# Eight loads in flight instead of four, and branch steps a place later, in a two-layer gated model

## The chip, the cores and the metric

One core of a Trainium2 chip runs the whole program. The metric is device microseconds of one execution; the kernel before took 1480.65 us, the median of three runs (1479.81 to 1485.36). The profiled execution took 1480.23 us, its span is 1478.6 us.

## The reference

Two layers, each a recurrent mixing step and a feed-forward part, both behind a gain:

```python
x = x + tanh(g_xattn[0]) * wkv(w, u, layernorm(x), ctx)
x = x + tanh(g_ffn[0])   * dense(layernorm(x), W1, W2, W3)
x = x + tanh(g_xattn[1]) * wkv(time_decay, time_first, layernorm(x), ctx)
x = x + tanh(g_ffn[1])   * experts(layernorm(x), gate_w, w1, w2, w3)
```

x is 8 x 256 x 512, that is 2048 tokens. `wkv` is a decaying weighted mean over the 256 steps of a sequence: sum of exp(k) v over sum of exp(k), with a bonus for the step itself. `dense` is `silu(x W1') * (x W3')`, 2048 wide, then a Walsh-Hadamard transform and W2. `experts` routes each token to two of eight experts by a gate and adds `silu(h1) * h3` times w2, weighted.

## The kernel before

The tokens are four groups of 512, x lies in SBUF as `X`, four rows of four tiles (a row for each group). All large matmuls are done in f16 with every operand split into a high and a low half, three products each.

**Three parts.** A prologue prepares the dense weights and group 0. Then come 64 *chunks*: chunk n = 16 g + j does slice j of the 2048 hidden columns for group g. An epilogue does the last group's second mixing step and the routing, and then the expert slots run, bound by TensorE.

**A chunk.** TensorE does an A group and a B group of 12 up matmuls each (L983, bank A and bank B), then the 12 down matmuls of the chunk before (L995). ScalarE (ACT) takes silu of bank A into `sg` (L532), VectorE (DVE) multiplies it with bank B (L819, the *product*), ACT casts it to its high half `hs` (L540) and DVE makes the low half (L823). The next A group waits for silu, the next B group for the product, the down group for the low half. Each engine has one instruction order, fixed when the program is built.

**Branches.** Beside the chunks run mixing steps of other groups: `("pre", g)` is the first layer's mixing of group g, `("post", g)` the second layer's. `FIRST` gives a branch's first chunk, F here. `STEPS` gives each step's chunk after F and its place: place 0 is ahead of the chunk's up matmuls and its silu, place 1 is behind them. On DVE both places lie ahead of the product. In order: `stats` (DVE) and `r0` (ACT, logarithm and exponential of the variance), `newton`; `norm` (ACT, writes `A`); `kT0/kT1`, eight transposes each on TensorE (L955); `e0/e1` (ACT, exp); `k0`, `k1`, `den`, `num`, `mix` (DVE, the scans and products; L677 begins k0, L683 k1, L643 den, L637 num, L696 mix); `ln`, `rec` (ACT); `yT0/yT1` (transposes of `V`, L960); `add0/add1` (DVE, with new statistics); `r2`, `newton2`, `norm2`; `xT0/xT1` (L955); `xh`, `xl` (the halves of the result on ACT and DVE); for a post branch `last` (TensorE, the gate's logits, L966) and `raw`, and then the gate steps `gate1`, `gate1b`, `gate2`, `rank`, `ranked` at the chunks of `GATES`. In chunk 16 g + 1 DVE also adds the dense result of group g - 1 to x (`resid`, L831).

**Units.** The experts' weights are 192 *units* of 128 x 512 f32 in DRAM. Each is loaded (SP, L285), cast to its high half by ACT (L433), its low half is made by DVE (L804), and both are stored as f16 (SP, L289). `UNITS` says how many a chunk does. The first of a chunk stands ahead of silu on ACT and ahead of the product on DVE, the second between silu and `hs` and between the product and the low half, the others last. The loads land in `raw`, a ring of four; SP issues in turn the store of unit u and the load of unit u + 4. `LATE` gives the chunks in which a piece of the dense weights is still cast (`w_high`, `w_low`), staged in rows 2 and 3 of `X`, which their x can only enter afterwards.

## Time and profile before

| | us |
|---|---|
| median of three runs | 1480.65 |
| profiled execution | 1480.23 |
| its span | 1478.6 |
| first up matmul of chunk 0 | 111.88 |
| first up matmul of chunk 63 | 732.50 |
| residual add of the last group | 745.62 |

The page says of the whole span: PE 1242.8 us busy (84%), DVE 727.5 (49%), ACT 505.4 (34%), POOL 202.7 (14%). PE's tenths in the 40 slices are lower in the slices of the dense chunks than in those of the expert slots, and its clock is 8 or 9 tenths in many of them. The start times below are microseconds from the span's start. A group of matmuls printed as one row has its start and its length; since matmuls overlap, the pace is to be taken from one start to the next.

### The profile page before, as it was taken

Reading aid. Unit: us, or ns where it says so; the run is one execution under the profiler, and the core shown is the slowest. Engines: PE = TensorE matmul, PEld = TensorE weight load, DVE = VectorE, ACT = ScalarE, POOL = GpSimd, SP = SyncE. Lnnn points to the kernel's source line nnn. Section 1 sums busy time; section 2 is a strip of 40 time slices with the busy share of each in tenths; the row PEclk is TensorE's granted clock in tenths of the full one; section 3 lists DMA queues with packets and bytes.
Section 4 is the critical chain, followed back from the end, with each engine's and each line's share of the span. In section 5 each row is a group of like instructions: output and inputs, shape, how many; then the busy total and the mean of one; then the engine's idle time right before and its main releaser. Section 6 shows DMA issues by size and latency. Waiting matters only on the chain. (4 is left out here: it accounts for less than half of the span.)

```text
span 1478.6 us, 19663 instructions
## 1 busy us (share of the span) xinstructions
PE 1242.8 (84%) x5785; PEld 590.7 (40%) x5786; DVE 727.5 (49%) x1175; ACT 505.4 (34%) x671; POOL 202.7 (14%) x206
## 2 busy tenths in 40 slices
PE   1278798899899898988924099999999999999995
PEld 0034344344454444534513044444444444444442
DVE  6957967868679587795665312122122121221221
ACT  3337557466463675545432011111111111111110
POOL 0000000000003000030200322322122223222232
PEclk9989999999999999999965589999999999999998
DMA  6024577455662656627777078696989896945333
GB/s 253 29 114 162 195 252 260 138 167 173 209 210 58 192 191 213 200 78 246 230 204 238 18 157 197 138 185 147 146 177 191 183 191 146 192 80 102 76 68 61
DMA packets 228344, 239.11 MB, mean 162 GB/s; under 512 B 137168, under 2 KB 141520, under 8 KB 225168
## 3 DMA queue, kind: packets, MB, share of 16 engines
q1 hardware_dynamic: 84816, 163.53, 34.7%
q10 hardware_dynamic: 130512, 52.70, 19.8%
q0 software_dynamic: 12960, 22.15, 8.0%
q8 instruction: 32, 0.52, 0.2%
q14 instruction: 24, 0.20, 0.0%
HBM read 138.68 MB, written 69.65 MB: 141 GB/s over the span
## 5 line engine op out<-in xcount | busy, mean ns | idle before, releaser
L1058 PE MATMUL PS<-weights,xs 128*128 x1872 | 413.1, 381 | 30.0 <-DMA xs<-X 30.0
L983 PE MATMUL PS<-xs,weights 128*128 128x512 f16 x1536 | 359.4, 391 | 27.6 <-DVE sg L819 16.5
L1058 PEld LDWEIGHTS PS<-weights,xs 128*128 128x128 f16 x1872 | 183.8, 98 | 252.9 <-issue 33.9
L983 PEld LDWEIGHTS PS<-xs,weights 128*128 128x128 f16 x1536 | 153.0, 101 | 223.9 <-issue 26.8
L886 DVE SCALAR_TENSOR_TENSOR A<-A,PS 128x1024 f32<-128x1024 f32 x39 | 47.6, 1221 | 349.0 <-PE PS L1058 325.7
L995 PE MATMUL PS<-weights,hs 128*128 128x512 f16 x768 | 182.1, 388 | 1.2 <-DVE hs L823 1.2
L578 ACT ACTIVATE A<-PS 128x1024 f32<-128x1024 f32 x39 | 39.9, 1023 | 322.8 <-PE PS L1058 197.0
L337 POOL DMA_INDIRECT row_list<-entry,pos x32 | 39.6, 1238 | 792.2 <-DVE pos L769 461.4
L804 DVE SCALAR_TENSOR_TENSOR halves<-raw,halves 128x512 f16<-128x512 f32 x192 | 128.9, 686 | 37.9 <-ACT halves L433 37.2
L433 ACT ACTIVATE halves<-raw 128x512 f16<-128x512 f32 x192 | 115.7, 618 | 40.4 <-DMA raw<-ew 37.2
L995 PEld LDWEIGHTS PS<-weights,hs 128*128 128x128 f16 x768 | 76.4, 100 | 88.1 <-issue 7.2
L897 DVE TENSOR_SCALAR V<-PS,outl 128x512 f32<-128x512 f32 x39 | 29.3, 751 | 164.6 <-PE PS L1072 149.4
L1072 PE MATMUL PS<-weights,SQ 128*128 x480 | 106.7, 379 | 0.0
L586 ACT ACTIVATE E<-A 128x1024 f16<-128x1024 f32 x39 | 41.2, 1056 | 189.6 <-DVE A L886 169.0
L1072 PE MATMUL PS<-weights,xs 128*128 x456 | 101.6, 379 | 3.9 <-DMA xs<-E 3.1
L955 PE MATMUL PS<-idn,A 128*128 128x128 f32 x256 | 44.8, 333 | 69.2 <-ACT A L479 63.0
L373 POOL DMA_INDIRECT out<-V,outl x39 | 68.8, 1764 | 199.8 <-DVE V L897 192.4
L540 ACT ACTIVATE hs<-sg 128x512 f16<-128x512 f32 x64 | 40.2, 627 | 142.4 <-DVE sg L819 142.4
L1072 PEld LDWEIGHTS PS<-weights,SQ 128*128 128x128 f16 x480 | 47.0, 98 | 56.6 <-issue 1.0
L955 PEld LDWEIGHTS PS<-idn,A 128*128 128x128 f32 x256 | 37.6, 173 | 78.5 <-issue 67.7
L1072 PEld LDWEIGHTS PS<-weights,xs 128*128 128x128 f16 x456 | 44.5, 98 | 58.4 <-issue 7.4
L1013 PE MATMUL PS<-weights,hads 128*128 128x512 f16 x128 | 32.3, 417 | 41.6 <-DVE weights L789 41.6
(144 smaller groups left out, 1024.3 us busy)
## 6 DMA issues: line engine op xcount, KB each, us to landing
raw<-ew SPq DMA_DIRECT2D x192, 256.0 KB, 3.8
e<-halves SPq DMA_DIRECT2D x192, 256.0 KB, 3.0
weights<-e SPq DMA_DIRECT2D x96, 512.0 KB, 4.8
V<-ctx_cm ACTq DMA_DIRECT2D x7, 1024.0 KB, 5.5
X<-w ACTq DMA_DIRECT2D x4, 1024.0 KB, 6.0
out<-X ACTq DMA_DIRECT2D x4, 1024.0 KB, 9.7
xn_rows<-SQ ACTq DMA_DIRECT2D x8, 512.0 KB, 4.1
X<-w2t SPq DMA_DIRECT2D x3, 1024.0 KB, 10.7
```

The source lines that it names most:

```text
L373: gp.indirect_dma_start(out, bass.IndirectOffsetOnAxis(ap=outl[:, par, 0:1], axis=0), yt[par], None, compute_op=ADD).then_inc(ysto[par], 16)
L433: act.activation(halves[:, u % RING, 0, :], raw[:, u % RING, :], ACT.Copy, scale=SW).then_inc(s["unit_hi"], 1)
L540: act.activation(hs[:, n % 2, 0, :], sg[:, n % 2, :], ACT.Copy).then_inc(s["hh_done"], 1)
L578: act.activation(sil[0], h1, ACT.Silu, scale=1.0 / (SW * SX)).then_inc(s["sil_done"], 1)
L586: act.activation(hid[par][:, :, 0, :], act8, ACT.Copy).then_inc(s["aT_used"], 1)
L804: ve.scalar_tensor_tensor(halves[:, u % RING, 1, :], raw[:, u % RING, :], SW, halves[:, u % RING, 0, :], MUL, SUB).then_inc(s["unit_lo"], 1)
L886: ve.scalar_tensor_tensor(sil[1], sil[0], SH / (SW * SX), h3, MUL, MUL).then_inc(s["act_done"], 1)
L955: ins = te.transpose(bank(S0 + c - a)[:, i * P:(i + 1) * P], A1[:, i * D + c * P:i * D + (c + 1) * P], idn[:, :])
L983: ins = te.matmul(bank(bk), wj[:, j, w, a, c * P:(c + 1) * P], xs[:, g % 2, b, c, :], start=(k == 0 and c == 0), stop=(k == 2 and c == C - 1))
L995: ins = te.matmul(bank(OUT0 + i), hs[:, n % 2, b, i * P:(i + 1) * P], wj[:, j, 2, a, :], start=j == 0 and k == 0, stop=j == J - 1 and k == 2)
L1058: ins = te.matmul(bank(n), xTt[k][:, b, c, :], weights_of(off, 2 * I // NT * c + n, a), start=(c == 0 and m == 0), stop=(c == C - 1 and m ...
L1072: ins = te.matmul(bank(6 + k % 2), aTt[k][:, b, c, :], weights_of(off, 2 * C * I // U + c, a), start=(c == 0 and m == 0), stop=(c == IC - ...
```

## The change

Four things are edited. The places of units (`unit_places`, new): besides the four of `raw`, four tiles of row 3 of `X` are lent from the end of chunk 9 until chunk 26, and four of row 0 from chunk 31 on, when group 0 is done with them. Each unit's load goes to the place that has been free the longest, and is issued by SP behind the store of the unit that was there, or the first time behind the last store of the chunk that frees it. SP's loop is unrolled, and x of group 3 is loaded by SP behind the last unit that used row 3, where ACT had issued it. `UNITS` is a new table; no unit stands ahead of silu any more, the first comes between silu and `hs`, all others last. `STEPS`: norm, kT0, k0, yT0, xT0, xT1, the x halves, last and raw come one place or one chunk later. `FIRST`, `GATES` and `LATE` are moved to match.

```diff
-FIRST = {("pre", 1): 0, ("pre", 2): 11, ("post", 0): 20, ("pre", 3): 30, ("post", 1): 39, ("post", 2): 49}
-GATES = {0: (31, 32, 34, 34, 35), 1: (50, 51, 53, 53, 54), 2: (60, 61, 62, 61, 62)}
-LATE = {1: 2, 2: 3, 4: 4, 7: 5, 9: 6, 10: 7}
+FIRST = {("pre", 1): 0, ("pre", 2): 10, ("post", 0): 20, ("pre", 3): 30, ("post", 1): 39, ("post", 2): 49}
+GATES = {0: (34, 40, 41, 42, 43), 1: (53, 58, 59, 59, 59), 2: (61, 62, 63, 63, 63)}
+LATE = {1: 2, 2: 3, 4: 4, 6: 5, 8: 6, 9: 7}
...
-STEPS = [("stats", 0, 0), ("r0", 0, 0), ("newton", 0, 0), ("norm", 1, 0), ("kT0", 1, 1), ("e0", 2, 0), ("k0", 2, 0),
+STEPS = [("stats", 0, 0), ("r0", 0, 0), ("newton", 0, 0), ("norm", 1, 1), ("kT0", 2, 0), ("e0", 2, 0), ("k0", 3, 0),
...
-         ("yT0", 6, 1), ("add0", 7, 0), ("yT1", 7, 1), ("add1", 8, 0), ("r2", 8, 0), ("newton2", 8, 0), ("norm2", 8, 1),
-         ("xT0", 9, 0), ("xh0", 9, 0), ("xl0", 9, 0), ("xT1", 9, 1), ("xh1", 10, 0), ("xl1", 10, 0), ("last", 10, 1),
-         ("raw", 11, 0)]
+         ("yT0", 7, 0), ("add0", 7, 0), ("yT1", 7, 1), ("add1", 8, 0), ("r2", 8, 0), ("newton2", 8, 0), ("norm2", 8, 1),
+         ("xT0", 9, 1), ("xh0", 10, 0), ("xl0", 10, 0), ("xT1", 10, 1), ("xh1", 11, 0), ("xl1", 11, 0), ("last", 11, 1),
+         ("raw", 12, 0)]
...
+LEND, LENT, GIVEN = max(LATE), 26, 31
+
+def unit_places():
+    done = list(itertools.accumulate(n for row in UNITS for n in row))
+    last = [-1] * RING + [done[LEND] - 1] * 4 + [done[GIVEN] - 1] * 4
+    uses, places = [0] * (RING + 8), []
+    for u in range(NU):
+        open_ = [k for k in range(RING + 8) if last[k] < u - 1 or k < RING]
+        if u >= done[LENT]:
+            open_ = [k for k in open_ if not RING <= k < RING + 4]
+        k = min(open_, key=lambda k: (last[k], k))
+        places.append((k, uses[k], last[k]))
+        uses[k], last[k] = uses[k] + 1, u
+    return places
...
-            with sp.Fori(0, NU // RING - 1, 1) as m:
-                for k in range(RING):
-                    store_unit(RING * m + k, k)
-                    load_unit(RING * m + RING + k, k)
+            def load_units(ahead):
+                for u, (k, use, after) in enumerate(PLACES):
+                    if after == ahead:
+                        if k == RING and use == 0:
+                            sp.wait_ge(s["w_lo"], NW)
+                        if k == RING + 4 and use == 0:
+                            sp.wait_ge(s["x3_out"], 16)
+                        sp.dma_start(raws[k], ew[u * P:(u + 1) * P, :]).then_inc(unit_in[k], 16)
+            for u in range(NU):
+                sp.wait_ge(s["unit_lo"], u + 1)
+                sp.dma_start(e16[u * P:(u + 1) * P, :], ...).then_inc(unit_out[u % RING], 16)
+                load_units(u)
+                if u == lent:
+                    sp.dma_start(xg(3), x_tm[3, :, :]).then_inc(x_in[3], 16)
...
                 if n in LATE:
                     w_high(LATE[n])
-                for u in units[0:1]:
-                    unit_high(u)
                 act.activation(sg[:, n % 2, :], bank(ABANK), ACT.Silu, ...)
                 for step in steps_beside(g, j, 1):
                     run(*step)
-                for u in units[1:2]:
+                for u in units[0:1]:
                     unit_high(u)
...
                 act.activation(hs[:, n % 2, 0, :], sg[:, n % 2, :], ACT.Copy)...
-                for u in units[2:]:
+                for u in units[1:]:
                     unit_high(u)
```

DVE's chunk is edited in the same way. The units of a branch's chunks F + 2 to F + 6 were 4, 4, 1, 2, 4 for post 0 and are 4, 0, 3, 4, 4.

TensorE, chunks 28 to 30, before (L983 is the up group of a chunk, L995 a down group, L955 are xT0 and xT1 of post 0, L966 its logits):

```order
L983 MATMUL PS<-xs,weights 128x512 x24
L995 MATMUL PS<-weights,hs 128x512 x12
L955 MATMUL PS<-idn,A 128x128 x8
L983 MATMUL PS<-xs,weights 128x512 x24
L955 MATMUL PS<-idn,A 128x128 x8
L995 MATMUL PS<-weights,hs 128x512 x12
L983 MATMUL PS<-xs,weights 128x512 x24
L966 MATMUL PS<-gw,E 128x8 x16
```

The same chunks after, with L1005, L1017 and L977 for the three kinds:

```order
L1005 MATMUL PS<-xs,weights 128x512 x24
L1017 MATMUL PS<-weights,hs 128x512 x12
L1005 MATMUL PS<-xs,weights 128x512 x24
L977 MATMUL PS<-idn,A 128x128 x8
L1017 MATMUL PS<-weights,hs 128x512 x12
L1005 MATMUL PS<-xs,weights 128x512 x24
L977 MATMUL PS<-idn,A 128x128 x8
L1017 MATMUL PS<-weights,hs 128x512 x12
```

xT0 moved behind the up group of chunk 29, xT1 behind that of chunk 30, and the logits are in chunk 31.

ACT, from silu of chunk 38 to silu of chunk 40, before (L532 silu with its table, L479 the norm, L433 units, L540 `hs`, L504 a half of x, L452 to L464 the logarithm step of post 1):

```order
L532 ACTIVATE sg<-PS 128x512
L479 ACTIVATE A<-X,rt 128x512 x4
L433 ACTIVATE halves<-raw 128x512
L540 ACTIVATE hs<-sg 128x512
L504 ACTIVATE xs<-PS 128x1024
L452 ACT_TABLE_LOAD
L463 ACTIVATE rt<-mv,eps 128x4
L464 ACTIVATE rt<-rt 128x4
L433 ACTIVATE halves<-raw 128x512
L532 ACT_TABLE_LOAD
L532 ACTIVATE sg<-PS 128x512
```

After, from the second silu (chunk 39) to the norm behind silu of chunk 40 (L557 silu, L460 units, L565 `hs`, L544 and L545 the exponentials of gate1b, L531 a half of x, L506 the norm of post 1):

```order
L557 ACTIVATE sg<-PS 128x512
L460 ACTIVATE halves<-X 128x512
L565 ACTIVATE hs<-sg 128x512
L460 ACTIVATE halves<-X 128x512 x3
L544 ACT_TABLE_LOAD
L544 ACTIVATE q<-q 128x32
L545 ACTIVATE q<-q 128x32
L531 ACTIVATE xs<-PS 128x1024
L557 ACT_TABLE_LOAD
L557 ACTIVATE sg<-PS 128x512
L506 ACTIVATE A<-X,rt 128x512 x4
```

The unit ahead of silu is gone, the exponentials and a half of x stand ahead of silu of chunk 40, and the norm came behind it.

DVE, from the units behind the low half of chunk 22 to the product of chunk 24, before (L804 units, L677 and the first L637 are k0, L683 to L643 k1, L819 the product, L823 the low half, the last two den):

```order
L677 TENSOR_TENSOR V<-E,V 128x1024
L637 SCALAR_TENSOR_TENSOR SQ<-dec,E 128x256 x4
L804 SCALAR_TENSOR_TENSOR halves<-raw,halves 128x512
L819 SCALAR_TENSOR_TENSOR sg<-sg,PS 128x512
L804 SCALAR_TENSOR_TENSOR halves<-raw,halves 128x512
L823 TENSOR_TENSOR hs<-sg,hs 128x512
L804 SCALAR_TENSOR_TENSOR halves<-raw,halves 128x512 x2
L683 TENSOR_TENSOR V<-E,V 128x1024
L637 SCALAR_TENSOR_TENSOR SQ<-dec,E 128x256 x4
L643 SCALAR_TENSOR_TENSOR E<-E,eu,SQ 128x2x255 x2
```

After (L828 units, L701 and the first L661 are k0, L707 to L667 k1, L841 and L845 product and low half of chunk 23):

```order
L828 SCALAR_TENSOR_TENSOR halves<-raw,halves 128x512 x3
L701 TENSOR_TENSOR V<-E,V 128x1024
L661 SCALAR_TENSOR_TENSOR SQ<-dec,E 128x256 x4
L707 TENSOR_TENSOR V<-E,V 128x1024
L661 SCALAR_TENSOR_TENSOR SQ<-dec,E 128x256 x4
L667 SCALAR_TENSOR_TENSOR E<-E,eu,SQ 128x2x255 x2
L841 SCALAR_TENSOR_TENSOR sg<-sg,PS 128x512
L845 TENSOR_TENSOR hs<-sg,hs 128x512
L667 SCALAR_TENSOR_TENSOR E<-E,eu,SQ 128x2x255 x2
L661 SCALAR_TENSOR_TENSOR A<-dec,V 128x256 x6
```

k0 moved from ahead of chunk 22's product to k1, and the units between are gone.

## Rows read from the trace of the kernel before

**Rows 1.** Windows: busy time per engine, granted clock, DMA share, GB/s.
```profile
core 0: us, PE busy (x) PEld busy (x) DVE busy (x) ACT busy (x) POOL busy (x), PEclk, DMA share, GB/s
111.00:746.00 635.00, 572.23 (x2712) 277.12 (x2712) 471.66 (x821) 364.09 (x517) 31.49 (x24) 0.95 0.58 187
```

**Rows 2.** Timeline of PE: start us, length us, line, operands; chunk starts and pace.
```profile
111.88 5.35 PE L983 MATMUL PS<-xs,weights 128*128 128x512 f16 x24 [3.21 <-DVE weights L799]
...
311.71 7.03 PE L983 MATMUL PS<-xs,weights 128*128 128x512 f16 x24
...
500.23 6.68 PE L983 MATMUL PS<-xs,weights 128*128 128x512 f16 x24
...
592.22 1.04 PE L955 MATMUL PS<-idn,A 128*128 128x128 f32 x8
593.09 2.75 PE L995 MATMUL PS<-weights,hs 128*128 128x512 f16 x12
595.68 5.34 PE L983 MATMUL PS<-xs,weights 128*128 128x512 f16 x24
600.86 3.63 PE L966 MATMUL PS<-gw,E 128*128 128x8 f32 x32
...
732.50 5.34 PE L983 MATMUL PS<-xs,weights 128*128 128x512 f16 x24
```

**Rows 3.** Waits of PE, 115 to 746: us in total, times, longest.
```profile
PE PS L955 <- ACT A L479: 22.2, 8, 5.1
PE PS L983 <- DVE sg L819: 16.5, 13, 2.5
PE PS L960 <- DVE V L697: 12.4, 6, 4.6
PE PS L983 <- ACT sg L532: 7.9, 3, 4.3
```

**Rows 4.** ACT's units (L433): duration ns, and what ACT waited for.
```profile
L433 ACT ACTIVATE halves<-raw x192: 612/615/631, 116.8 to 744.4; 128x512 f16<-128x512 f32 x192
...
  DMA raw<-ew: 37.2, 20
```

**Rows 5.** Timeline of DVE: scan steps of post 0, then gate1.
```profile
343.57 1.22 DVE L683 TENSOR_TENSOR V<-E,V 128x1024 f32<-128x1024 f32 x1 [1.72 <-ACT E L490]
...
347.30 1.41 DVE L643 SCALAR_TENSOR_TENSOR E<-E,eu,SQ 128x510 f32<-128x510 f32 x2
...
352.48 1.41 DVE L643 SCALAR_TENSOR_TENSOR E<-E,eu,SQ 128x510 f32<-128x510 f32 x2
...
357.43 0.69 DVE L804 SCALAR_TENSOR_TENSOR halves<-raw,halves 128x512 f16<-128x512 f32 x1
...
360.44 1.27 DVE L637 TENSOR_TENSOR_SCAN A<-dec,V 128x256 f32<-128x256 f32 x2
...
369.49 2.28 DVE L696 SCALAR_TENSOR_TENSOR SQ<-E,SQ 128x2048 f32<-128x2048 f32 x1
...
372.96 1.22 DVE L698 TENSOR_TENSOR V<-V,SQ 128x1024 f32<-128x1024 f32 x1
...
419.46 0.18 DVE L712 COPY q<-PS 128x32 f32<-128x32 f32 x1
...
422.14 0.69 DVE L804 SCALAR_TENSOR_TENSOR halves<-raw,halves 128x512 f16<-128x512 f32 x1
```

**Rows 6.** Timeline: from the stats to silu in chunk 20; half of xn.
```profile
314.11 0.68 DVE L630 BATCH_NORM_STATS2 st<-X 128x6 f32<-128x512 f32 x1
...
317.42 1.28 ACT L452 ACT_TABLE_LOAD   x1 [4.48 <-DVE mv L631]
...
319.78 1.28 ACT L532 ACT_TABLE_LOAD   x1
...
321.08 0.60 ACT L532 ACTIVATE sg<-PS 128x512 f32<-128x512 f32 x1
...
400.44 1.90 ACT L508 ACTIVATE SQ<-A 128x2048 f16<-128x2048 f32 x1
```

**Rows 7.** Timeline of DVE: the last group's residual add.
```profile
745.62 2.34 DVE L831 SCALAR_TENSOR_TENSOR X<-PS,sc,X 128x2048 f32<-128x2048 f32 x1
```

38 lines of the change are left out of this document (16 added, 22 removed), and 6 rows, old and new, of the table UNITS.

## The prediction

> **What bounds the kernel now.** I read the windows first. The kernel has three parts: the 64 dense chunks (111 to 746 us), an epilogue that belongs to one branch alone, and the expert slots. The dense part is 635 us of the span and PE is busy in 572 of them at a granted clock of 0.95 [rows 1]. The changed lines all lie in it, apart from names; so the sum is made there. Next the pace of PE: 24 up matmuls take 5.18 us from first start to the next group's start, eight transposes 0.87, twelve down matmuls 2.59 [rows 2]. A chunk at full rate is therefore 5.18 + 2.59 = 7.77 us, a branch adds six groups of transposes (5.2 us), and each of the three gates' logit matmuls 3.5 (600.86 to the next group). Then the chunk starts [rows 2] against that pace. From chunk 0 to 20 there are 20 chunks, less the down group that chunk 0 lacks, and 11 transposes: 155.4 - 2.6 + 9.6 = 162.4, measured 199.8, lost 37.4. From 20 to 39 (12 transposes, one logit group): 147.6 + 10.4 + 3.5 = 161.5, measured 188.5, lost 27.0. From 39 to 49 (7): 77.7 + 6.1 = 83.8, measured 95.5, lost 11.7. From 49 to 63 (6, two logit groups): 108.8 + 5.2 + 7.0 + 0.4 = 121.4, measured 136.8, lost 15.4. All told 91 us are lost. The waits of PE explain 60 of them: transposes of A on the norm 22.2, of V on mix 12.4, up matmuls on the gate product (`sg`) 16.5, and on silu 7.9 [rows 3]. The rest is mostly the half clock behind a wait: 24 matmuls that take 5.34 us at 2.4 GHz take 7.03 at 311.71 and 6.68 at 500.23, behind transposes that had waited on the norm [rows 2]; so one such drop to 1.2 GHz costs 1.3 to 1.7 us in the up group alone. So PE bounds the dense part, and what counts is how late ACT and DVE are at these four hand-overs. ACT's own waits for raw units, 37.2 us in 20 places [rows 4], hurt only where it has no slack.
>
> **Part 1, transposes a place later.** Each transposed group now stands behind 5.18 or 2.59 us more of matmuls, and nothing is added to PE. The norm waits (22.2, longest 5.1) for xT0 go: the norm follows silu at once on ACT and is shorter than the up group of 5.18 that now lies between. Of the V waits (12.4) 2.6 us each are covered. But `k0` moves from chunk F+2 (F is the first chunk of a branch) into F+3, beside `k1`. With DVE's prices [rows 5] I follow one branch. k0 is a product and four scans, as k1's first two rows, 3.73 (343.57 to 347.30). k1 takes 5.06 (343.57 to 352.48, less a `sg`, an `hs` and four units at 0.61 each and a wait of 0.2), den 4.95 (352.48 to 357.43), num 6.40 (360.44 to 369.49, less `sg`, `hs`, two units and the wait, 2.65), mix 4.6 (3.5 to the second half's product at 372.96, when the first half of V is ready, and 1.15 for that). DVE is free about 1.4 us into F+3 (three units behind `hs`); k0 and k1 end at 10.2, and `sg` must end by 5.18 + 5.18 to keep the next B group in time: 0.45 late. F+4 (den) is in time, having 3 units instead of the four on both sides of before. F+5: 20.6 + 6.40 = 27.0 against a product that may start at 25.7: 1.3 late. F+6 has had four units behind it: V's half is ready at 34.4, PE is there at 32.8: 1.6. Two small ones follow, 0.4 (yT1 on the add) and 0.6 (silu behind `r2`). That is 4.35 us a branch, and DVE, not PE, paces F+3 to F+6, so a half clock inside it is mostly absorbed. Before, the same branch at 25 to 29 waited longer and clocked down twice.
>
> **Part 2, no unit before silu.** A unit of 0.62 on ACT [rows 4] goes from in front of silu, and one like it on DVE from in front of `sg`. It is worth 0.6 us only in a chunk where silu or `sg` ends last. Those are the first chunks of the branches: stats from 314.11 until ACT goes on at 317.42 (3.3), then table load, logarithm, unit, table load and silu, which ends at 321.68 [rows 6]: 4.27 us, now 3.65. The unit is not dropped, it comes behind `hs`, where it lies beside matmuls.
>
> **Part 3, what the new places collide with.** At F+10 the transposed halves (`xh0`, `xl0`) now stand in the same place as the next branch's stats and r0, in front of silu. Behind a pre branch these are 1024 elements on either engine, half of what takes 1.9 and 2.3 us, and cost 1 us of stall (chunk 20). Behind a post branch ACT has 1.0 + 1.9 [rows 6] and DVE 2.3 (as mix's first row [rows 5]) ahead of the stats: ACT is done at 2.9, DVE with its low half at 5.2, the stats end at 8.5, silu 3.65 later at 12.1, while PE gets to the next A group at 5.18 + 0.87 + 2.59 = 8.65. Stall 3.4 at chunk 30; 4.4 at 49, where the residual add of 2.3 [rows 7] stands too; each with a half clock of 1.7. At 39 nothing lies between `r2` of one branch (chunk 38) and the next's stats: silu of chunk 38 ends as chunk 39 starts, then come norm2 (four slices, 2.9 as an estimate from 1.9 for 2048 elements and a start-up each), a unit, `hs`, the low half and two units, so DVE is free at 6.2, + 3.3 + 3.65 = 13.1 against 8.7: stall 4.3 again. And `gate1b` of post 0 in front of silu in chunk 40 adds the exponentials, two table loads of 1.28 and a chain of eight small DVE operations (1.8, by gate1's twelve in 2.7, 419.46 to 422.14 [rows 5]), so that the norm behind it ends 3.1 us after kT0 is due (half clock included). In the first ten chunks the weight staging comes a chunk earlier: w_high (1.9) and w_low (2.3) fall beside den, mix and `r2`. Followed with the same prices, DVE's chain gives stalls of 0.75, 1.65, 0.55, 0.95, 0.55 and 1.45 at chunks 4 to 8. Then silu of chunk 8 has `r2` (add1 ends 4.9, + 1.85), w_high 1.9, table and silu in a row, 10.6 against 7.8: 2.8 at chunk 9; 1.0 at 10, where w_high waits for its piece, issued only behind chunk 8; and with that lateness and the next branch's stats 4.6 at 11.
>
> **Part 4, eight places for raw units.** A load has eight units of lead instead of four, some two chunks, so ACT's 37.2 us of raw waits go once the lent rows are in use (after chunk 9). On PE's way this is little: most of it lies beside matmuls. The clear gain is at the end: the residual add of the last group starts at 745.62, 13.1 after chunk 63's start [rows 2, 7], while 5.18 + 2 x 2.59 and the last units put it at 10.5; the units stand in front of `hs` and of the add and come late with their loads. Gain 2.6. Issuing the loads unrolled and queueing two row loads of X behind them on SP I price at 0; if a store had to wait behind such a load, at most a few us once, and a gain there has no mechanism.
>
> **The sum.** Lost after: 0 to 20: 3.3 (chunk 0: wait 1.6 with half clock) + 5.9 (to chunk 8) + 8.4 + 1.7 x 2 + 6.6 (pre 2, with the residual add in chunk 17) + 1.4 half clock = 29.0, saves 8.4. 20 to 39: 1.0 + 4.35 + 3.4 + 1.7 + 0.9 (half clock behind the logits) + 8.0 (pre 3: the residual add 2.35 and gate1 2.7 join the scans) + 1.0 = 20.3; one transposed group fewer falls in the stretch (0.9): saves 7.5. 39 to 49: 4.3 + 3.1 + 7.1 + 0.7 = 15.2: costs 3.5. 49 to 63: 4.4 + 1.7 + 0.9 + 7.4 + 0.7 + 1.7 + 1.0 = 17.8, and one group of transposes more: costs 3.3. End: saves 2.6. Net 8.4 + 7.5 - 3.5 - 3.3 + 2.6 = 11.7. The profiled execution took 1480.23 us (span 1478.6), 0.4 under the median of the three runs; 1480.65 - 11.7 = 1469. Epilogue and expert slots keep their time.
>
> **A rule of the Trainium skill weighed.** In this trace a table load takes 1.28 us and the silu behind it starts 0.02 later [rows 6]; the instruction order has four more of them now, all about gate1b, at chunks 40 and 58. The Trainium skill ("ScalarE: Activation LUTs", What ACT_TABLE_LOAD costs) puts a switch at 1.28 plus a drain of 1.38. By that page the four switches would cost 5.5 us more on ACT, of which about 3 reach PE at 40 and 58, and the time would be 1472. The row shows no such drain, so I go by the row.
>
> **Rivals.**
> Full slack. DVE and ACT are less late than I add up, and the moved transposes and the loads' lead take away the 22.2 + 12.4 us of waits for the norm and for V [rows 3] with most of their half clock, while the new collisions cost only half of my 20 us. For it: these are the two largest of the removable waits. Against it: DVE's scan chain has barely slack. Gain 25, time 1455.
> No change. The stalls only change their names: the norm waits become silu waits one chunk on. For it: at 39 PE goes on without a silu wait, but at its start it had waited on the norm, up to 5.1 us [rows 3], so that silu had that much more time. If each of the six scan chains runs 1 us later than I say, 6 us of the 12 are gone: 1475.
> Slower. The mechanism is the logarithm in front of silu in the crowded chunks 10, 30, 39, 40 and 49. If DVE reaches the stats 2 us later there than I say (units of the chunk before, four instead of three), each stall grows by 2 and draws a half clock of 2.5 instead of 1.7, and kT0 behind it waits as well: 5 x (2 + 0.8 + 0.8) = 18 more, 1487. It decides from 3.3 us a chunk on.
> A longer table switch. If a table load holds ACT longer than its row says, the four added ones come late in front of silu at 40 and 58: 1472 by the Trainium skill's drain, of which no row speaks.
>
> **Chances.** Forecast 1469 (1462 to 1476): 0.55. Full slack 0.13, no change 0.15, slower 0.14, the page's 0.03. A measurement of this kernel tells about 0.5% from no change, that is below 1473.2 or above 1488.1. Forecast's own spread puts three quarters under 1473.2: faster 0.42 + 0.13 = 0.55, same 0.13 + 0.12 + 0.03 + half of the slower case (it ends at 1487 with as much below as above 1488) 0.05 = 0.33, slower 0.12 with the tails. Range 1455 to 1484, which leaves out about 2 in 10.
>
> **What would show it.** Right: no PE wait on the norm over 1 us save kT0 at chunk 41; PE waits on silu grow from 3 to some eight, at chunks 1, 9 to 11, 31, 40, 50 and 59, sum over 20 us; waits on V stay at five or six with about 1.6 each; raw waits of ACT under 10 us; granted clock of 111 to 735 about 0.95 or a little above; residual add 10.5 after chunk 63 starts. Wrong: if silu waits at 31, 40 and 50 are missing (full slack), or if `sg` waits in F+4 exceed 2 us in every branch (DVE chain underrated).

## The result and the profile after

The changed kernel took 1499.89 us (median of five runs, 1496.72 to 1502.1), the one before 1485.36 (five runs, 1479.81 to 1488.54): a ratio of 1.0108, 95% interval 1.0084 to 1.0132. It is 1.1% slower, where 1469 us was forecast. The profiled execution has a span of 1498.3 us, 19.7 more than before. The medians are only 14.5 apart: the profiled execution of before (1480.23) was one of its faster ones, so some 5 of the 19.7 us are chance.

The windows first. The dense part now lasts until 764.65 us instead of 745.62. PE is busy in it for 2.3 us less than before [rows 1] with as many matmuls, and its clock is a shade higher, so all of the loss is waiting.

```profile
111.00:765.00 654.00, 569.94 (x2712) 273.12 (x2712) 471.77 (x823) 368.80 (x524) 22.90 (x20) 0.96 0.58 182
```

The waits of PE and of ACT's units, 115 to 762 us (in total, times, longest):

```profile
PE PS L1005 <- ACT sg L557: 33.3, 11, 5.8
ACT halves L460 <- DMA e<-halves: 27.9, 13, 8.3
PE PS L1005 <- DVE sg L841: 13.2, 13, 2.0
PE PS L982 <- DVE V L721: 12.3, 6, 5.6
PE PS L977 <- DVE xs L733: 8.9, 3, 7.1
ACT halves L460 <- DMA raw<-ew: 5.1, 4, 1.9
PE PS L993 <- ACT E L533: 4.9, 1, 4.9
```

Against [rows 3] the 22.2 us on the norm are gone, and those on silu grew from 7.9 to 33.3. Against [rows 4] ACT's 37.2 us for raw units are 5.1, but it now waits 27.9 for its *stores* (e from halves). And two waits are new in kind: transposes of A on `xs` (L733, the low half of a branch's result), and the rank matmuls (L993) on `E`. Both are waits for the engine that still reads the two side PSUM banks. The rank step was also moved, which the list of the change does not say: in `GATE_STEPS` it went from place 1 to place 0, ahead of its chunk's up matmuls.

All of PE's waits come to 81.1 us here, and to 60.2 before (115 to 746). The four hand-overs that the prediction reckoned with (norm, V, product, silu) are 58.8 of them, and were 59.0 [rows 3]. So the norm's waits were traded for silu's, and the growth in sum lies outside the four: 22.3 us instead of 1.2. Of these, 19.3 are waits for a reader of the side banks (8.9 on `xs`, 7.1 on `E`, 3.3 on the add, which reads yT0).

PE's timeline holds the chunk starts of [rows 2] (chunks 0, 20, 39, 49 and 63 are the first, second, third, eighth and last row) and the worst place:

```profile
113.54 5.35 PE L1005 MATMUL PS<-xs,weights 128*128 128x512 f16 x24 [3.21 <-DVE weights L823]
...
300.15 5.34 PE L1005 MATMUL PS<-xs,weights 128*128 128x512 f16 x24
...
487.77 5.35 PE L1005 MATMUL PS<-xs,weights 128*128 128x512 f16 x24 [0.44 <-ACT sg L557]
...
500.59 7.04 PE L1005 MATMUL PS<-xs,weights 128*128 128x512 f16 x24 [4.01 <-ACT sg L557]
...
520.01 1.97 PE L977 MATMUL PS<-idn,A 128*128 128x128 f32 x8 [7.12 <-DVE xs L733]
521.77 6.82 PE L1005 MATMUL PS<-xs,weights 128*128 128x512 f16 x24
...
534.30 0.18 PE L993 MATMUL PS<-a,tris 128*128 128x8 f16 x1 [2.25 <-ACT E L517]
...
602.48 5.34 PE L1005 MATMUL PS<-xs,weights 128*128 128x512 f16 x24
...
617.09 6.93 PE L1005 MATMUL PS<-xs,weights 128*128 128x512 f16 x24 [5.81 <-ACT sg L557]
...
752.46 5.35 PE L1005 MATMUL PS<-xs,weights 128*128 128x512 f16 x24
```

So 0 to 20 takes 186.6 us (before 199.8), 20 to 39 187.6 (188.5), 39 to 49 114.7 (95.5) and 49 to 63 150.0 (136.8); DVE's residual add starts 12.2 after chunk 63 (13.1, [rows 7]):

```profile
764.65 2.35 DVE L853 SCALAR_TENSOR_TENSOR X<-PS,sc,X 128x2048 f32<-128x2048 f32 x1 [1.06 <-PE PS L1017]
```

Chunk 0 starts 1.7 us later, and what follows the add takes 733.7 instead of 733.0. The sum: -13.2 - 0.9 + 19.2 + 13.2 - 0.9 + 1.7 + 0.7 = 19.8, but for rounding the difference of the spans. All of the loss lies behind chunk 39, apart from 9 us at 30 to 33 that 33 to 39 and 20 to 30 give back.

**Chunk 30** takes 14.3 us (392.43 to 406.75), because its silu is late. ACT's last two units of chunk 29 wait 1.26 and 1.28 us for their loads, so ACT is done with its part of `xh0` at 397.41, 5.0 us into the chunk instead of the 2.9 forecast, and DVE, which waits for it, begins `xl0` and the stats only then:

```profile
394.07 0.63 ACT L460 ACTIVATE halves<-raw 128x512 f16<-128x512 f32 x1 [1.28 <-DMA raw<-ew]
...
397.44 2.29 DVE L728 SCALAR_TENSOR_TENSOR SQ<-A,SQ 128x2048 f16<-128x2048 f32 x1 [2.02 <-ACT SQ L535]
```

At chunk 49 ACT is as late, behind two units that wait 0.86 and 1.27 us for stores.

**Chunk 40** (500.59 to 521.77, 21.2 us where 7.8 is full pace) shows two more causes, the side banks and the gate in front of silu. ACT, then DVE:

```profile
503.55 1.28 ACT L544 ACT_TABLE_LOAD   x1
506.22 0.23 ACT L544 ACTIVATE q<-q 128x32 f32<-128x32 f32 x1 [1.38 <-DVE q L767]
...
506.48 1.00 ACT L531 ACTIVATE xs<-PS 128x1024 f16<-128x1024 f32 x1
507.50 1.28 ACT L557 ACT_TABLE_LOAD   x1
508.79 0.60 ACT L557 ACTIVATE sg<-PS 128x512 f32<-128x512 f32 x1
510.39 2.93 ACT L506 ACTIVATE A<-X,rt 128x512 f32<-128x512 f32 x4 [1.00 <-issue]
...
515.83 1.00 ACT L531 ACTIVATE xs<-PS 128x1024 f16<-128x1024 f32 x1
```

```profile
516.89 0.18 DVE L779 TENSOR_TENSOR q<-q 128x32 f32<-128x32 f32 x1
...
518.73 1.23 DVE L733 SCALAR_TENSOR_TENSOR xs<-PS,xs 128x1024 f16<-128x1024 f32 x1
```

The gate's exponentials with two table loads and the first half `xh0` stand ahead of silu (508.79), norm and `hs` behind it, and only then, in front of chunk 41's silu, comes `xh1` at 515.83; on DVE `gate2` (516.89) stands ahead of `xl1`, which ends at 519.96. PE could have filled kT0 of post 1 from 513.3 on, when the norm that it reads ended, but there are only two side PSUM banks, S0 and S1, for all transposes and gate matmuls: kT0 goes into them when `xl1` has read xT1 out of them. PE stood from 512.9 to 520.0, of which the norm alone would have cost 0.4.

**The stores.** When the last gate step knows a group's places in the routing, GpSimd (POOL) issues eight indirect DMAs, the *scatter*: 1024 entries of 8 bytes into `row_list`. In the changed kernel:

```profile
546.12 1.52 POOL L364 DMA_INDIRECT row_list<-entry,pos  x1 [545.49 <-DVE pos L793]
...
556.27 1.42 POOL L364 DMA_INDIRECT row_list<-entry,pos  x1 [0.30 <-issue]
```

The second group's begin at 712.89. The windows behind the two, and the DMA issues in 540 to 575 and in 575 to 610 (KB each, median us from issue to landing):

```profile
557.00:572.00 15.00, 10.62 (x49) 4.42 (x47) 10.85 (x12) 3.09 (x6) 0.69 (x1) 1.00 1.07 135
725.00:740.00 15.00, 13.58 (x77) 7.63 (x76) 3.21 (x5) 1.89 (x3) 0.00 (x0) 1.00 1.12 129
```

```profile
e<-halves SPq DMA_DIRECT2D x7, 256.0 KB, 8.6
...
e<-halves SPq DMA_DIRECT2D x14, 256.0 KB, 3.1
```

The DMA engines are fully busy and move 129 to 135 GB/s; a store takes 8.6 us instead of 3.1. In the first window the packets of q1, the queue of the units, take 105.5% of the 16 engines' time for 2.02 MB, the scatter's own (q0) 1.1%:

```profile
q1 hardware_dynamic: 1106, 2.02, 105.5%
```

So it is the units' packets that get long. ACT stands at those two places, with the next silu queued behind its units (at 569.36 and 741.08):

```profile
568.83 0.63 ACT L460 ACTIVATE halves<-X 128x512 f16<-128x512 f32 x1 [2.42 <-DMA e<-halves]
...
734.55 0.63 ACT L460 ACTIVATE halves<-X 128x512 f16<-128x512 f32 x1 [8.30 <-DMA e<-halves]
```

### The profile page after: what moved, and what is told of

The parts are those of the page before. It is cut to its first block and busy times, and to the rows that moved or that the text cites. A ratio compares the mean times of both kernels' runs of the same rounds, so it can differ in the third digit from the quotient of the medians.

```text
span 1498.3 us, 18666 instructions
## 1 busy us (share of the span) xinstructions
PE 1245.2 (83%) x5785; PEld 588.5 (39%) x5786; DVE 726.0 (48%) x1175; ACT 508.7 (34%) x675; POOL 198.8 (13%) x206
## 5 line engine op out<-in xcount | busy, mean ns | idle before, releaser
L1005 PE MATMUL PS<-xs,weights 128*128 128x512 f16 x1536 | 360.2, 392 | 49.7 <-ACT sg L557 33.3
L1005 PEld LDWEIGHTS PS<-xs,weights 128*128 128x128 f16 x1536 | 152.1, 100 | 246.0 <-ACT sg L557 38.7
L1017 PE MATMUL PS<-weights,hs 128*128 128x512 f16 x768 | 180.6, 386 | 1.5 <-DVE hs L845 1.5
L602 ACT ACTIVATE A<-PS 128x1024 f32<-128x1024 f32 x39 | 39.9, 1023 | 309.2 <-PE PS L1080 211.9
L364 POOL DMA_INDIRECT row_list<-entry,pos x32 | 35.6, 1113 | 815.3 <-DVE pos L793 545.5
L1017 PEld LDWEIGHTS PS<-weights,hs 128*128 128x128 f16 x768 | 76.2, 100 | 89.3 <-issue 5.2
L828 DVE SCALAR_TENSOR_TENSOR halves<-raw,halves 128x512 f16<-128x512 f32 x116 | 76.7, 685 | 30.5 <-ACT halves L460 30.5
L977 PE MATMUL PS<-idn,A 128*128 128x128 f32 x256 | 41.6, 316 | 55.0 <-ACT A L506 39.9
L565 ACT ACTIVATE hs<-sg 128x512 f16<-128x512 f32 x64 | 40.1, 627 | 138.4 <-DVE sg L841 133.4
L841 DVE SCALAR_TENSOR_TENSOR sg<-sg,PS 128x512 f32<-128x512 f32 x64 | 43.7, 683 | 72.6 <-PE PS L1005 53.2
L460 ACT ACTIVATE halves<-raw 128x512 f16<-128x512 f32 x116 | 68.4, 617 | 11.6 <-DMA e<-halves 6.5
L1094 PEld LDWEIGHTS PS<-weights,xs 128*128 128x128 f16 x456 | 45.3, 99 | 59.9 <-issue 9.4
L1035 PE MATMUL PS<-weights,hads 128*128 128x512 f16 x128 | 33.4, 427 | 41.6 <-DVE weights L813 41.6
```

The costliest lines, as they stand in the source:

```text
L460: act.activation(halves[:, u % RING, 0, :], raws[PLACES[u][0]], ACT.Copy, scale=SW).then_inc(s["unit_hi"], 1)
L565: act.activation(hs[:, n % 2, 0, :], sg[:, n % 2, :], ACT.Copy).then_inc(s["hh_done"], 1)
L828: ve.scalar_tensor_tensor(halves[:, u % RING, 1, :], raws[PLACES[u][0]], SW, halves[:, u % RING, 0, :], MUL, SUB).then_inc(s["unit_lo"], 1)
L841: ve.scalar_tensor_tensor(sg[:, n % 2, :], sg[:, n % 2, :], SH / (SW * SX), bank(BBANK), MUL, MUL).then_inc(s["hid_done"], 1)
L977: ins = te.transpose(bank(S0 + c - a)[:, i * P:(i + 1) * P], A1[:, i * D + c * P:i * D + (c + 1) * P], idn[:, :])
L1005: ins = te.matmul(bank(bk), wj[:, j, w, a, c * P:(c + 1) * P], xs[:, g % 2, b, c, :], start=(k == 0 and c == 0), stop=(k == 2 and c == C - 1))
```

## The experiments

Sixteen kernels were run. "After" is the changed kernel. Ratios are to the kernel before on the same chip, with 95% intervals; before's medians there were 1483.8 to 1485.7. The stretches are differences between the starts of A groups in each profile; "tail" is from chunk 63 to the residual add, "rest" what follows. They are of one profiled execution each, the time is a median. e12 and e15 are the same up to e15's first scatter (452.64), and differ by up to 1.7 us in the stretches before it: less than 2 us in a stretch says nothing.

| | us | ratio | 0-20 | 20-30 | 30-33 | 33-39 | 39-42 | 42-49 | 49-52 | 52-58 | 58-60 | 60-63 | tail | rest |
|---|---|---|---|---|---|---|---|---|---|---|---|---|---|---|
| before | 1485.4 | | 199.8 | 96.8 | 30.2 | 61.5 | 28.5 | 67.0 | 30.2 | 61.6 | 21.5 | 23.5 | 13.1 | 733.0 |
| after | 1499.9 | 1.0108 | 186.6 | 92.3 | 39.4 | 55.9 | 46.8 | 68.0 | 38.6 | 54.0 | 24.3 | 33.1 | 12.2 | 733.7 |
| e1 | 1509.8 | 1.0177 | 185.7 | 93.2 | 39.1 | 56.2 | 46.3 | 71.0 | 41.0 | 55.0 | 24.2 | 34.9 | 13.8 | 733.0 |
| e2 | 1481.4 | 0.9975 | 199.7 | 96.6 | 30.2 | 62.1 | 28.5 | 66.6 | 30.2 | 62.3 | 22.7 | 23.6 | 10.6 | 731.7 |
| e3 | 1491.6 | 1.0049 | 186.6 | 87.2 | 42.5 | 55.9 | 46.2 | 64.5 | 35.0 | 54.0 | 24.1 | 31.1 | 12.2 | 733.6 |
| e4 | 1497.5 | 1.0084 | 186.9 | 92.1 | 39.5 | 55.9 | 39.9 | 68.6 | 40.3 | 54.1 | 24.7 | 34.5 | 12.2 | 733.5 |
| e5 | 1498.6 | 1.0084 | 189.4 | 91.7 | 37.2 | 55.9 | 40.5 | 68.3 | 40.2 | 54.0 | 27.0 | 32.6 | 12.2 | 733.5 |
| e6 | 1504.9 | 1.0113 | 186.7 | 92.7 | 39.6 | 72.3 | 40.5 | 60.9 | 40.5 | 68.6 | 19.0 | 28.7 | 10.6 | 733.3 |
| e7 | 1494.8 | 1.0055 | 186.4 | 87.6 | 38.2 | 56.1 | 45.3 | 69.3 | 40.2 | 54.0 | 24.6 | 31.5 | 12.2 | 733.2 |
| e8 | 1488.0 | 1.0016 | 189.5 | 90.2 | 39.4 | 61.9 | 41.6 | 61.5 | 40.2 | 60.5 | 18.1 | 27.0 | 10.6 | 731.7 |
| e9 | 1488.2 | 1.0016 | 186.6 | 92.6 | 39.8 | 55.9 | 46.6 | 62.2 | 40.1 | 54.5 | 24.3 | 27.0 | 10.6 | 737.6 |
| e10 | 1484.6 | 0.9985 | 189.6 | 90.1 | 38.9 | 60.4 | 35.6 | 61.5 | 40.8 | 59.0 | 18.1 | 28.7 | 10.6 | 738.4 |
| e14 | 1477.2 | 0.9958 | 199.4 | 96.7 | 30.2 | 58.3 | 28.5 | 66.6 | 28.5 | 61.2 | 22.7 | 23.5 | 10.6 | 734.1 |
| e13 | 1487.2 | 1.0004 | 190.3 | 94.4 | 28.5 | 59.7 | 37.1 | 73.8 | 30.2 | 58.1 | 27.5 | 27.4 | 12.2 | 735.5 |
| e11 | 1471.5 | 0.9912 | 187.0 | 102.2 | 30.2 | 58.8 | 28.5 | 69.0 | 28.5 | 60.7 | 21.5 | 23.5 | 10.6 | 737.9 |
| e12 | 1463.7 | 0.9852 | 190.2 | 94.6 | 28.5 | 59.4 | 28.0 | 68.1 | 28.5 | 57.4 | 21.4 | 23.7 | 10.6 | 737.8 |
| e15 | 1471.1 | 0.9915 | 191.7 | 93.5 | 30.2 | 64.0 | 27.6 | 67.9 | 28.5 | 60.0 | 21.7 | 23.7 | 10.6 | 734.0 |
| e16 | 1461.3 | 0.9849 | 190.2 | 94.7 | 28.5 | 59.4 | 27.9 | 68.0 | 28.5 | 59.6 | 22.0 | 23.7 | 10.6 | 734.1 |

### Tables or ring: e1 and e2

e1 is after with the old ring of four raw units; e2 is after's twelve places with all tables and unit places of before.

```
e1: RING = 4 loads as before;  UNITS, STEPS, FIRST, GATES, LATE of after; no unit ahead of silu
e2: PLACES, load_units of after;  UNITS, STEPS, FIRST, GATES, LATE of before; first unit ahead of silu
```

> The changed kernel's tables (steps, first chunks, gates, units, no unit ahead of silu) with the old ring of four places. Theory S (the new step places cost the time: the half-products of x and the gate steps hold the two side banks and stand in front of silu at chunks 30 to 31, 39 to 42, 49 to 50): still slower than before by 10 to 16 us, chunk 40 about 21 us long; ACT waits for raw loads again (30 to 40 us) instead of for stores. Theory R (eight loads in flight push the stores back, and ACT waits for stores): at most 3 us slower than before, store waits under 8 us, since loads and stores alternate again.

Measured 1.0177 (1.0143 to 1.0212), 24 us over before and so more than either theory had; raw waits 51.4 us in 30 places.

> The kernel before with the lent places alone: its tables, its first unit ahead of silu, but eight places for raw units and the unrolled issue. Theory S: 0 to 5 us faster than before, raw waits of ACT under 8 us, store waits below 10. Theory R: 6 to 12 us slower than before, ACT's waits for stores 20 us or more.

Measured 0.9975 (0.9956 to 0.9995): the tail falls from 13.1 to 10.6 us as Part 4 had it. The tables lose 1.8% with the old ring and 1.3% with the places; the places give 0.7% back with them and 0.25% without. In e2 ACT still waits 14.6 us for stores, which before's trace does not show; e14 below, the same kernel with the scatters late, has no such wait.

### Who must wait for a store: e3 and e7

e3 shares the eight lent places, four for raw units and four for halves:

```
-raws = [raw ...] + X rows 3 and 0, tiles 0-3
+raws = [raw ...] + X rows 3 and 0, tiles 0,1;  halves = [halves ...] + X rows 3 and 0, tiles 2,3
```

> The changed kernel, with each lent row shared out: two tiles to raw units, two to the stores' halves, so six places for either. Theory R: the store waits of 27.9 us nearly vanish (under 6) and the time falls by 8 to 13 us against the changed kernel, most at chunks 45, 61 and 62. Theory S: 2 to 5 us faster than the changed kernel at most, chunk 40 stays at 21 us. If the DMA engines themselves are the limit when a chunk does four units, the waits only turn into raw waits of the same sum.

Measured 1.0049 (1.0026 to 1.0073). That is 8.3 us less than after, the low end of theory R. The store waits are gone, and twelve waits for loads, 24.6 us, took their place (after has 5.1). The longest, 10.8 us at 728.91, is where after waited for its stores behind the second scatter:

```profile
ACT halves L474 <- DMA raw<-ew: 12.7, 9, 5.4
ACT X L474 <- DMA X<-ew: 11.9, 3, 10.8
```

e7 is after with the first unit ahead of silu and of the product again.

> The changed kernel with the first unit of each chunk in front of silu and of the gate product again and the second behind silu, as before; tables and the lent places stay as changed. Theory B (with no unit in front, up to three units stand in a row behind the high half of the hidden rows, and their stores come due together, so ACT waits for the store of four units ago): ACT's waits for stores fall from 27.9 us to under 12 in sum and the longest from 8.3 to under 3, but each of the crowded first chunks gets 0.6 later; sum: 2 to 5 us faster than the changed kernel in chunks 42 to 49 and 60 to 63, 2 slower elsewhere; 1495 to 1498. Rival (the store waits come from loads queued eight ahead and not from the bunching): waits for stores stay above 20 us and the first chunks get later, 1501 to 1504.

Measured 1.0055 (1.0032 to 1.0079), faster than after, but not for the reason given: the store waits rose to 44.4 us in 20 places (115 to 790). Its gain is at 20 to 30 (87.6 us against 92.3). So taking the first unit from in front of silu and of the product, which is Part 2, cost time here; why is not settled.

### The side banks and the halves: e4 and e5

```
e4: ("xh1", 11, 0), ("xl1", 11, 0) -> ("xh1", 10, 1), ("xl1", 10, 1)
e5: e4 and ("xh0", 10, 0), ("xl0", 10, 0) -> ("xh0", 9, 1), ("xl0", 9, 1)
```

> The changed kernel with one step moved back: the second half of x (xh1, xl1) stands behind silu of chunk F+10 and no longer in chunk F+11. Theory S: kT0 of post 1 in chunk 41 no longer waits 7.1 us for xl1; chunk 40 shrinks from 21.2 to 15 to 17 us, and 4 to 8 us are saved against the changed kernel; chunk 30 and 49 stay long (14.3, 14.6). Rival: the norm, which ends at 513.2 of that chunk, and DVE's backlog are what kT0 would wait for next: under 2 us saved.

Measured 1.0084 (1.0057 to 1.0112). The bank's wait goes and 39 to 42 falls by 6.9; kT0 of post 1 now waits 1.4 us, on the norm. From 42 to 63 the kernel gives 4.2 back, while its store waits grow from 27.9 to 33.5. The time is 2.4 us less, which the intervals do not tell from after:

```profile
ACT halves L460 <- DMA e<-halves: 33.5, 17, 9.7
...
PE PS L977 <- DVE xs L733: 1.6, 1, 1.6
```

> The changed kernel with the halves of the transposed rows of each branch earlier: the first (xh0, xl0) behind silu of chunk F+9 instead of in front of silu of F+10, the second (xh1, xl1) behind silu of F+10 instead of in front of silu of F+11. Nothing else is moved. Theory C (crowded first chunks: the halves stand in front of the next branch's stats and logarithm in chunks 10, 20, 30, 40, 49): silu of chunks 30 and 49 ends about 3 us sooner after the chunk's start (14.3 and 14.6 in the changed kernel), the wait of the next up group falls from 5.5 and 5.8 to 2 to 3, and chunks 30 to 33 and 49 to 52 fall from 39.4 and 38.6 us by about 4 each; with the side banks free in time as well (chunks 39 to 42 fall from 46.8 to about 40, as with xh1 alone), the time falls by 10 to 14 us against the changed kernel, to about 1487. Rival: the lateness is the vector engine's own backlog and only moves; then chunks 30 to 33 and 49 to 52 keep their 39 us, the halves delay the gate product of chunks F+9 by 1 to 2 us, and the time is 1495 to 1500.

Measured 1.0084 (1.0057 to 1.0111), as the rival had it: 30 to 33 falls by 2.2 only, 49 to 52 rises. The silu waits at chunks 31 and 50 do shrink, from 5.5 and 5.8 us to 3.4 and 2.6, but others come: kT0 of post 1 waits 3.3 on the norm, yT0 7.1 on mix. Taking the halves alone out of the first chunk's way does not mend it.

### The gates: e6, and all three at once: e8

```
-GATES = {0: (34, 40, 41, 42, 43), 1: (53, 58, 59, 59, 59), 2: ...}
+GATES = {0: (32, 33, 35, 35, 36), 1: (51, 52, 54, 54, 55), 2: ...}
```

> The changed kernel with the gates of posts 0 and 1 put right behind their logits again (chunks 32 to 36 and 51 to 55 instead of 34 to 43 and 53 to 59); the rest is as changed. Theory G (the gates are what fills chunks 40 to 43 and 58 to 60): chunk 40, 21.2 us in the changed kernel, loses the two table loads, two exponentials and eight small operations in front of its silu, some 6 us, and the wait of chunk 42 for the rank (2.25) and of 59 (4.9) go; chunks 39 to 42 fall from 46.8 to about 39 and 58 to 60 from 24.3 to 22; chunks 33 to 39 and 52 to 58 grow by about 2 each; time down by 5 to 7, to about 1493. Rival (side banks and the second branch's scans decide, gates only add where there is room): chunk 40 still waits for the low half of xT1 in chunk 41, 39 to 42 falls by less than 3 us, and 33 to 39 and 52 to 58 grow by as much as is won: 1498 to 1502.

Measured 1.0113 (1.0066 to 1.016). 39 to 42 and 58 to 60 fell by 6.3 and 5.3 as expected, 42 to 49 by 7; but 33 to 39 and 52 to 58 grew by 16.4 and 14.6. The gate steps now stand beside k0 and k1, the product of chunk 34 keeps PE waiting for 5.0 us, and the scatter begins at 471.53. (The rank step keeps its new place 0.) The windows and ACT's rows of the kernel with the gates back, then PE's:

```profile
480.00:490.00 10.00, 10.00 (x52) 4.92 (x51) 3.88 (x8) 1.38 (x3) 2.94 (x4) 1.00 1.08 100
490.00:500.00 10.00, 1.87 (x9) 0.67 (x7) 4.03 (x6) 1.03 (x2) 0.00 (x0) 0.83 1.15 85
```

```profile
486.47 0.63 ACT L460 ACTIVATE halves<-X 128x512 f16<-128x512 f32 x1 [7.79 <-DMA e<-halves]
```

```profile
504.22 2.31 PE L1005 MATMUL PS<-xs,weights 128*128 128x512 f16 x5 [12.35 <-ACT sg L557]
```

Here the picture showed itself: behind the scatter, in chunks 37 and 38 here and in 44, 45, 60 and 61 of after, DMA is full at 85 to 135 GB/s, the stores come late, and the silu behind the units with them. That is theory D.

> The changed kernel with three edits at once: the lent rows shared between raw units and halves (two places each), the halves of the transposed rows earlier, and the gates right behind their logits. If the three causes are separate their savings add: 8 (store waits) + 10 (halves early, banks free) + 4 (gates) = 22 less than the changed kernel's 1499, so about 1477, 0.5% faster than before and the fastest of all. If they overlap, as store waits came back when the halves alone were moved, half of that: 1488, slower than before. Chunks 39 to 42: 46.8 us in the changed kernel, 34 or less if additive; 30 to 33: 39.4, 35 or less; 49 to 52: 38.6, 33 or less.

e8 joins e3, e5 and e6. 1487.99 us, 1.0016 (0.9994 to 1.0038): the savings overlap. Against the additive case it is 11 us late, and PE's longest wait on silu, behind chunk 39 and just after the scatter, is 11.0.

### The scatters: e9, e10 and e14

```
+gp.wait_ge(s["resid_done"], NG)      # GpSimd, ahead of the scatters
 for g in range(NG):
     scatter(g)
```

> The changed kernel with the routing list's scatters (eight indirect DMAs of tiny packets for each group of tokens, issued on GpSimd as soon as a group's places are known) all held back until the last residual add; nothing else is moved. In the changed kernel the scatters of posts 0 and 1 are issued at 546 to 557 us and at 713 to 725, and for 10 to 15 us after each the DMA engines are 0.9 to 1.5 busy at only 76 to 200 GB/s, and the scalar engine waits 6.2 and 14.1 us for stores. Theory D (the store waits of chunks 44 to 46 and 60 to 62 come from the scatters, whose place moved with the gates): both go; waits for stores fall from 27.9 us to under 10, chunk 45 falls from 16.0 us to about 11.5, chunks 42 to 49 from 68.0 to about 64, chunks 60 to 63 from 33.1 to 26 to 28, and the time falls by 7 to 12 us to about 1489; the epilogue hides the 31 us of scatters issued late. Rival (the stores bunch behind the high half of the hidden rows whatever the scatters do): waits for stores stay above 20 us and the time within 3 us of 1499; if the late scatters reach the expert slots, the part after the last residual add grows from 734 us by up to 25 and the time with it.

Measured 1.0016 (0.9991 to 1.0041), 0.9% under after. Windows at the same places of chunks 44 and 60, and the waits, of after with the scatters late:

```profile
556.00:571.00 15.00, 13.13 (x65) 6.12 (x64) 14.59 (x17) 4.34 (x8) 0.00 (x0) 1.00 0.58 192
720.00:735.00 15.00, 15.00 (x85) 8.51 (x85) 9.53 (x25) 6.48 (x11) 0.00 (x0) 1.00 0.65 226
```

```profile
PE PS L1006 <- ACT sg L558: 32.8, 11, 6.4
...
ACT halves L461 <- DMA e<-halves: 10.5, 10, 3.7
```

The same queues move 192 GB/s at a share of 0.58 and 226 at 0.65, against 135 at 1.07 and 129 at 1.12. In the first window the units' queue needs 57.8% of the engines' time for 2.88 MB:

```profile
q1 hardware_dynamic: 1588, 2.88, 57.8%
```

A store issued in 540 to 575 lands after 2.9 us there. 42 to 49 falls by 5.8, 60 to 63 by 6.1, and the rest grows by 3.9, where 24 late scatter DMAs now stand ahead of the last group's eight; e16 bears that out. The longest wait on V, 5.6 us, is 1.5. Nothing else was moved, so theory D is shown for after. The silu waits stay, they have another cause, and so do 10.5 us of store waits.

> The combined kernel (lent rows shared, halves earlier, gates right behind their logits) with the scatters held back until the last residual add. The combined kernel's scatters begin at 471 us, and behind them the scalar engine waited 2.2 and 4.9 us for raw units in chunk 39, which took 19.9 us; its stats were 5 us late. Theory D: chunk 39 falls to about 14.5 and chunk 50's wait stays; time 1480 to 1483, about before's. Rival: chunk 39 is late for the vector engine's own backlog; within 2 us of 1488.

0.9985 (0.9961 to 1.0009): 39 to 42 falls from 41.6 to 35.6 and the rest grows by 6.7. The time lies between theory and rival, and its interval overlaps with that of e8.

> The kernel with the tables and unit places of before and the twelve raw places (1481.4 us, run earlier) with the scatters held back until the last residual add. Theory D says what before paid for its own scatters at 461 and 649 us: ACT's unit waits of 7.4 and 6.4 us behind them go, of which PE sees 2 to 4 (chunks 33 to 39 and 52 to 58, 62 us each), and the part after the last residual add grows by 4 to 6 as it did in the changed kernel: 1481 to 1484, no gain. Rival (the scatters cost before as much as the changed kernel, 11 us): 1474 to 1477.

1477.19 us, 0.9958 (0.9941 to 0.9976), against 0.9975 of e2; the intervals overlap. 33 to 39 falls from 62.1 to 58.3, the rest grows from 731.7 to 734.1. From chunk 0 to the last residual add it takes 6.9 us less than e2 (626.2 against 633.1), where e9 takes 11.0 less than after (640.1 against 651.1). No gain was expected: the places of before pay for their scatters too, less than after's, but more than theory D had allowed, and the time is just outside the rival's range.

### The ends of the branches: e13, e11 and e12

e13 undoes one part of after, the places from xT0 on:

```
-("xT0", 9, 1), ("xh0", 10, 0), ("xl0", 10, 0), ("xT1", 10, 1), ("xh1", 11, 0), ("xl1", 11, 0), ("last", 11, 1), ("raw", 12, 0)
+("xT0", 9, 0), ("xh0", 9, 0), ("xl0", 9, 0), ("xT1", 9, 1), ("xh1", 10, 0), ("xl1", 10, 0), ("last", 10, 1), ("raw", 11, 0)
```

> The changed kernel with one part of it undone: xT0, its halves, xT1, its halves, the logits and the raw step of every branch at the places of before (F+9 to F+11). The later norm, kT0, k0 and yT0, the gates at 34 to 43 and 53 to 59, the units and their twelve places, and the scatters right behind the routing stay as changed. Theory (the ends of the branches lose by running into the next branch's first chunks, apart from gates and scatters): 30 to 33 falls from 39.4 us to 28 to 31, 49 to 52 from 38.6 to 28 to 31, 39 to 42 from 46.8 to 36 to 39 (the gate's exponentials are still in front of silu in chunk 40), while the waits of xT0 on the norm come back at chunks 28, 38, 47 and 57 (about 4 us and a half clock each: 20 to 30, 33 to 39, 42 to 49 and 52 to 58 grow by 2 to 4 each); stores still wait 20 us or more behind the scatters. Time 1480 to 1486. Rival (the gates and scatters are the whole loss): 30 to 33 and 49 to 52 stay above 36 and the time at 1495 to 1500.

1487.17 us, 1.0004 (0.9981 to 1.0026), 1.0% under after and 1 us over its range. The waits of PE, 115 to 752 us:

```profile
PE PS L977 <- ACT A L506: 28.5, 7, 7.8
...
PE PS L1005 <- ACT sg L557: 5.7, 5, 1.6
```

30 to 33, 39 to 42 and 49 to 52 fall by 29.0 together, but about 16 of these are lost again in other stretches (1499.9 to 1487.2 is 12.7). Silu waits fall from 33.3 to 5.7 and norm waits come back with 28.5: between these two the waits only change their name. The four hand-overs come to 59.0 us, as in before and in after. What is gained are PE's other waits, the side banks' above all: 11.1 us instead of 22.3.

e11 keeps after's places for the first three branches only (post 0 up to its second norm), with the scatters late.

> The changed order for the first three branches only (pre 1, pre 2, and post 0 up to its second norm); from there and for pre 3, posts 1 and 2 the places of before, gates as before, each chunk's first unit in front of silu as before, raw units in the twelve places, units of the chunks adapted, and the scatters held back. Theory (the change's gain and loss are separate: 13 us won in the first twenty chunks, 4.5 in the next ten, and the loss all in the branch ends at 30, 39, 40 and 49 and the gates): chunks 0 to 20 take 187 us (before 199.8), 20 to 30 90 (96.8), 30 to 33 31 to 34, from 39 on as before; the time is 1462 to 1468. Rival (ACT and DVE are simply behind: what is won early is lost at the next branch, since units and staging left over must be done later): from 30 on it is 10 us longer than before, 1475 to 1480.

1471.54 us, 0.9912 (0.9878 to 0.9946), over the 1462 to 1468 expected. 0 to 20 takes 187 us, and from 30 to 63 it is as before within 3 us; but 20 to 30 takes 102.2, and PE waits 6.1 us on the norm in chunk 29. Four units a chunk stand beside mix and the add there; that this is the cause was not tested.

e12 has for every branch after's places up to norm2 and before's from xT0 on, gates as before, e3's sharing, units moved away from F+3 and the gates, and the scatters late.

> For every branch the changed places up to the second norm (norm, kT, k0, yT a place later) and those of before from xT0 to raw, gates as before, lent rows shared, units of the chunks adapted, scatters held back. Theory (the later transposes of the halves xT0 and xT1, which put the halves and the raw step into the next branch's first chunks, are the part that loses; the later kT0 and yT0 are the part that gains): 0 to 20 187 to 190 us, 30 to 33 32 to 35, 33 to 39 57 to 60, 39 to 42 31 to 34, 49 to 52 31 to 34, 52 to 58 56 to 59; time 1463 to 1472. Rival (the later k0, beside k1, collides with the gates there as it did in the kernel with the gates put back, 12 us at chunk 39 and 5 at 34): 1480 to 1490.

1463.7 us, 0.9852 (0.9812 to 0.9893), within its range. Its dense part and its waits, 115 to 726 us:

```profile
111.00:725.00 614.00, 558.54 (x2712) 272.65 (x2712) 471.74 (x823) 361.77 (x520) 0.00 (x0) 0.97 0.58 194
```

```profile
PE PS L994 <- ACT A L523: 27.2, 6, 7.9
PE PS L1022 <- DVE sg L858: 13.0, 12, 2.0
PE PS L999 <- DVE V L738: 5.2, 4, 1.5
...
PE PS L1022 <- ACT sg L574: 3.1, 3, 1.6
ACT halves L477 <- DMA raw<-ew: 2.7, 2, 2.0
```

Against e13 it lacks the gates in front of silu, among others: 39 to 42 is 9.1 less, 58 to 60 6.1. No store is waited for.

Against before the dense part is 23.2 us shorter, and only 8.4 of that are waits of PE (51.8 instead of 60.2). The same 2712 matmuls keep PE busy for 558.5 us instead of 572.2 [rows 1], at a granted clock of 0.97 instead of 0.95: some 14 us are matmuls that took longer before, at the lower clock. Which of the waits that went had drawn the clock down was not separated.

### When to scatter: e15 and e16

```
e15: e12 without the wait
e16: gp.wait_ge(s["down_done"], 41); scatter(0); scatter(1); gp.wait_ge(s["unit_lo"], NU); scatter(2), scatter(3)
```

> The fastest kernel so far (1463.7 us: first halves of the branches as changed, their ends and the gates as before, lent rows shared) with the scatters again right behind the routing instead of held back. Theory D: they start near 450 and 630 us, beside 4 units a chunk; stores and loads slow down for 10 to 15 us each, ACT waits 5 to 10 us more, 33 to 39 and 52 to 58 grow by 3 to 8 each, and the end gains the 4 back: 1464 to 1472. Rival (with two places more for units and halves nothing waits for the scatters): 1460.

0.9915 (0.9896 to 0.9933), 1471.07 us, as theory D had it; 33 to 39 grows by 4.6, 52 to 58 by 2.6, the rest falls by 3.8.

> The same fastest kernel with the first group's scatters released in chunk 42, where no unit stands, the second's right behind its routing (chunk 54, after two chunks without units), and the others when the last unit is converted. If the late scatters cost 4 us after the last residual add because 24 of them stand in front of the last group's, that part falls from 737.8 to about 733.5 us, and the dense part keeps its time within 1: 1459 to 1461. Rival: the scatters slow the units of chunks 43 and 55 and win nothing: 1463 to 1467.

1461.31 us (1460.29 to 1462.5), 0.9849 (0.983 to 0.9868): the fastest kernel, 1.5% under before. It has the rest back (734.1), and 52 to 58 gives 2.2 of it up again; the intervals don't tell it from e12.

## Why the prediction was wrong

**What bounds the kernel**: right that PE does. But its four hand-overs carry 59.0 of the 60.2 us of waits before and 58.8 of 81.1 after: reckoning by them alone could not see the loss. (The scatters sit in both: e9 has 5.5 us less in the four and 2.7 less outside.) Against the same pace the prediction had 29.0, 20.3, 15.2 and 17.8 us lost in its four stretches; the trace has 24.2, 27.0, 30.9 and 27.7.

**Part 1**, right in its mechanism. The norm waits went. Waits on V were to be five or six of 1.6 each; they are six and 12.3 us, one of 5.6, which is the scatter's (1.5 in e9). 0 to 20 saved 13.2 instead of 8.4: the scan chains and the weight staging cost less than added up, an error that hid part of the others.

**Part 2**, priced as a gain of 0.6 in a few chunks. e7 has it as a loss of 0.5% beside the rest of the change (1.0055 against 1.0108, intervals apart).

**Part 3 is the step that failed**, the list of what the new places collide with: two entries were missing from it and one was too small. First, the sizes of the crowded first chunks: silu ends 14.3 and 14.6 us after chunks 30 and 49 start, where 12.1 and some 13 were worked out, and at 39 12.8 (13.1). That is 2 us each, at two places, as the rival "slower" had it. The reason is ACT's units just before, which wait for a load or for stores; Part 4 took such waits to lie beside matmuls. Second, kT0 of post 1: 3.1 us with its half clock was forecast because of the norm; the norm ended 0.4 us after PE was there (with the bank free it is 1.4 in e4 and 3.3 in e5), and the wait of 7.1 with a half clock behind it came from a resource that the sum did not have, the two side banks. With nine chunks between pre 3 and post 1 and a branch that now ends at F+11 with its halves, one branch's kT0 and the other's `xl1` are in the same place of chunk 41; the reading of a bank is as much a wait as its filling. The rank matmuls in front of chunks 42 and 59 (2.25 and 4.9) are the same mistake. e4 takes the 7 us away, and e13 half of all waits outside the four hand-overs. Third, the gates: their last step releases eight DMAs on POOL's queue, and the sum moved the step without them. e13 (1.0%) and e9 (0.9%) each undo nearly the whole loss; the two were not undone together without other edits, so whether they add up exactly is open.

**Part 4** was right on raw waits (5.1, under 10 forecast) and on the end in e2 (10.6, forecast 10.5); in after itself the residual add comes 12.2 after chunk 63, with the last gate steps and the late units of chunk 62 in front of it (e9, with the same gate steps, has 10.6). Wrong was the price of 0 for the stores: with loads eight ahead, the halves' ring of four is what ACT waits for, 27.9 us. Sharing the lent places (e3) gives 0.6% back. But the longer ring of loads does not make these waits by itself: without the scatters they are 10.5 us (e9), and in the tables of before none (e14).

**The rule weighed.** The four added table loads come as the row had them: the load starts 0.02 us after the row ahead of it ends, takes 1.28 us, and silu starts 0.01 later (506.48, 507.50, 508.79 above). The Trainium skill's drain of 1.38 us ("ScalarE: Activation LUTs", What ACT_TABLE_LOAD costs) does not show here either; what is dear at chunk 40 is where the loads stand.

**The rivals.** "No change" told the kind of e13's trade (norm waits against silu waits), "slower" (0.14) the place; it gave 1487 for 3.6 us more at five chunks, and the time was 13 us over that, by the banks and the scatters, which no rival held. The range ended at 1484.

**The signs** asked for were nearly all there: no norm wait, silu waits over 20 us (33.3, though none over 1 us at chunks 10 and 59, and two of over 3 us at 21 and 62 that were not named), six waits on V, raw waits of 5.1, a clock of 0.96. Only the residual add was late, and the time was 31 us off. They named the waits that were expected, and none of them asked what PE waits for besides.

## What to carry to other kernels

When a step is moved, list for each thing it fills who must read it first, and what the step releases on other queues, DMAs above all; then look what stands in that chunk. Where a producer gets more buffers, look at the next ring behind it, and at what makes that ring slow. Add up all waits, not only those that were expected. A change of many moves is best split where one branch meets the next: here the later first halves of the branches, with their ends and gates left where they were and the scatters out of the way, ran 1.5% faster than before, and all of it together 1.1% slower.

## What the runs showed of the hardware

A scatter of 1024 entries of 8 bytes in eight indirect DMAs, 8 KB in all, holds up the other queues for 12 to 15 us after its last DMA is issued: 135 and 129 GB/s at DMA shares of 1.07 and 1.12, against 192 at 0.58 and 226 at 0.65 in the same chunks where it is not there (e9), and 8.6 us instead of 2.9 from the issue of a 256 KB store to its landing. The time is booked on the packets of the other queue, 105.5% for 2.02 MB against 57.8% for 2.88; the scatter's own take 1.1%. What in a scatter does this, no run shows. The Trainium skill ("DMA: Bandwidth & Descriptors", Issuing engines are not separate DMA queues) has DMAs of all issuers interleave on the same 16 engines; the trace agrees, since a scatter that GpSimd issues slows what SyncE issues, and adds the price. The profile charges these waits to the stores, not to the scatter.
